# Second layer norm and routing written as one stage, chunk by chunk, in a two-layer transformer kernel with a mixture of experts

## The reference, cut to what matters

```python
xn = _layernorm(x, axis=-1)
x = x + _L0_attn_ref(xn, ...) + _L0_ffn_ref(xn, L0_ffn_W1, L0_ffn_W2, L0_ffn_W3)
xn = _layernorm(x, axis=-1)
x = x + _L1_attn_ref(xn, ...) + _L1_ffn_ref(xn, L1_ffn_Wr, ...)
# inside the second layer
v = (x @ Wv)
probs = jax.nn.softmax(x @ Wr, axis=-1)
topw, topi = jax.lax.top_k(probs, K)
pos = (jnp.cumsum(oh, axis=0) * oh).sum(-1) - 1
```

## Time and profile before

| | us |
|---|---|
| median of 3 runs | 2762.9 (2759.66 to 2764.67) |
| span of the profiled execution, first to last instruction | 2757.8 |
| TensorE busy in the span | 2526.8 (92%) |
| VectorE busy in the span | 1757.1 (64%) |
| from the end of the first feed-forward's last sum to the next block after routing | 1331.3 to 1428.2 |

### The profile page before, as it was taken

One profiled execution on the slowest core, in us unless ns is written; L12 is line 12 of the kernel. 1 busy time (PEld: TensorE's weight loads), 2 busy tenths in 40 slices (PEclk: granted clock), 3 DMA queues, 4 the chain that ended last, 5 costly groups with the idle time before them and its releaser, 6 DMA issues. The chain is left out here.

```text
span 2757.8 us, 35900 instructions
## 1 busy us (share of the span) xinstructions
PE 2526.8 (92%) x12212; PEld 1711.0 (62%) x12212; DVE 1757.1 (64%) x4109; ACT 1080.5 (39%) x2566; POOL 1022.2 (37%) x756
## 2 busy tenths in 40 slices
PE   5889989898869999999697999978999979999998
PEld 2334434343348888888575777756777656667886
DVE  4647757575435555555545999956999923335886
ACT  2125535353522333222223777725777721111111
POOL 2217758584911111110003676624445410001442
PEclk9969999999979999999899999999999999999999
DMA  7371211111020000000211101010000078883201
GB/s 252 131 180 24 54 24 40 26 35 31 2 106 16 16 15 15 15 16 1 85 50 54 62 29 28 23 40 24 9 9 16 1 259 295 295 294 93 58 24 62
DMA packets 167335, 193.64 MB, mean 70 GB/s; under 512 B 51982, under 2 KB 114446, under 8 KB 166784
## 3 DMA queue, kind: packets, MB, share of 16 engines
q1 hardware_dynamic: 155648, 178.90, 20.8%
q0 software_dynamic: 11520, 12.64, 1.4%
HBM read 161.95 MB, written 54.53 MB: 78 GB/s over the span
## 5 line engine op out<-in xcount | busy, mean ns | idle before, releaser
L621 DVE TENSOR_REDUCE mx<-bank 128x1 f32<-128x512 f32 x512 | 327.9, 679 | 121.7 <-PE bank L528 115.5
L468 POOL TENSOR_TENSOR probs<-probs 128x1024 f32<-128x1024 f32 x128 | 301.5, 2376 | 211.2 <-PE bank L551 174.0
L679 ACT ACTIVATE probs<-bank 128x1024 f32<-128x1024 f32 x256 | 250.1, 1022 | 271.8 <-PE bank L541 271.8
L1475 POOL TENSOR_SCALAR mix<-mix,sm 128x256 f32<-128x256 f32 (+1 forms) x256 | 232.5, 919 | 175.1 <-DVE sm L1372 174.9
L1415 ACT ACTIVATE ms<-ms,sm 128x256 f32<-128x256 f32 (+1 forms) x512 | 247.6, 486 | 93.9 <-DVE sm L1343 92.9
L528 PE MATMUL bank<-k_parts,q_parts 96*128 96x512 f32 x512 | 219.8, 476 | 7.3 <-DVE X L644 3.3
L528 PEld LDWEIGHTS bank<-k_parts,q_parts 96*128 96x128 f32 x512 | 94.0, 196 | 171.4 <-DVE mx L621 139.1
L855 POOL TENSOR_TENSOR up_lo<-up_raw,up_hi 128x1024 fp32r<-128x1024 f32 x16 | 46.2, 2907 | 401.0 <-ACT up_hi L845 401.0
L1343 DVE CUSTOM_DVE_ANT_0 ms<-bank,misc 128x256 f32<-128x256 f32 (+1 forms) x512 | 184.7, 399 | 2.3
L541 PE MATMUL bank<-q_parts,k_parts 97*128 97x512 f32 x512 | 148.4, 406 | 15.8 <-ACT probs L679 8.9
L925 DVE TENSOR_TENSOR hid<-bank,sg 128x512 f32<-128x512 f32 x64 | 44.2, 691 | 180.2 <-ACT sg L875 180.2
(11 more groups left out here) (221 smaller groups left out, 5863.4 us busy)
## 6 DMA issues: line engine op xcount, KB each, us to landing
ewg<-in_L_ffn_Wg_dram SPq DMA_DIRECT2D x32, 704.0 KB, 6.8
ewu<-in_L_ffn_Wu_dram SPq DMA_DIRECT2D x32, 704.0 KB, 8.0
ewd<-in_L_ffn_Wd_dram SPq DMA_DIRECT2D x32, 512.0 KB, 5.2
q_parts<-qk_dram SPq DMA_DIRECT2D x48, 256.0 KB, 4.4
up_raw<-in_L_ffn_W_dram SPq DMA_DIRECT2D x16, 512.0 KB, 4.1
ewd<-in_L_ffn_Wd_dram SPq DMA_DIRECT2D x32, 192.0 KB, 5.3
qk_dram<-qk_hi SPq DMA_DIRECT2D x4, 1280.0 KB, 5.1
qk_dram<-qk_lo SPq DMA_DIRECT2D x4, 1280.0 KB, 7.2
```

What stands on the lines that cost most here:

```text
L468: pool.tensor_tensor(probs[:, even, half, :], probs[:, even, half, :], probs[:, odd, half, :], ALU.add).then_inc(S["paired"], 1)
L621: dve.reduce_max(mx[:, U % 2, q, h:h + 1], bank[:, h, :], AX.X).then_inc(S["max"], 1)
L679: act.activation(probs[:, s % BUFS, 2 * x:2 * x + 2, :], bank[:, 2 + 2 * x:4 + 2 * x, :], ACT.Exp, scale=scale).then_inc(S["exps"], 1)
L1475: pool.tensor_scalar(mix[:, p % 2, h, 0:w], mix[:, p % 2, h, 0:w], sm[:, p % 3, 8 + h:9 + h], None, ALU.mult).then_inc(S["probs"], 1)
```

## The change

The code that both layer norms shared is split. `layer_norm0` is the first one, with the same instructions as before. The second is written into `normalise_and_route`, one block in place of two:

- The statistics and aggregates of the second layer norm go into `swiglu`, last column group of the first feed-forward: behind the sum of each chunk stand 4 statistics and 4 aggregates. The aggregates are kept in the columns of the constant `had`, which is no longer needed by then.
- Variance plus epsilon, square root and reciprocal are done in 4 pieces of 4 tiles.
- TensorE's order is by chunks: transposes of the chunk's 4 tiles, some value products, logits of the chunk, turning of the logits of the chunk before. Value products 0 to 12 stand ahead of the count, 13 to 15 behind it.
- Banks: transposes use 3 banks in place of 4, the logits one (bank 3) in place of 4, the value products 2 (6 and 7) in place of 4.
- The 4 MB store of the normalised rows is 4 stores of 1 MB.

The core of the diff:

```diff
+                if last and a == 1:
+                    for s in range(SUBS):
+                        wait(dve, S["added"], (i * 2 + a) * (NC * SUBS) + c * SUBS + s + 1)
+                        dve.bn_stats(stats[:, s, :], X[:, c * SUBS + s, :]).then_inc(env["ln"][0], 1)
+                    for s in range(SUBS):
+                        dve.wait_ge(env["ln"][0], NT + c * SUBS + s + 1)
+                        dve.bn_aggr(env["moments1"][:, c * SUBS + s, :], stats[:, s, :]).then_inc(env["ln"][1], 1)
...
+                def turn_rows(n):
+                    pe.wait_ge(xn_ready, NT + n + 1)
+                    if n >= 3:
+                        pe.wait_ge(xt_taken, NT + n - 2)
...
+                def logits(c):
+                    if c == 0:
+                        pe.wait_ge(router_high, 4)
+                    pe.wait_ge(xt_taken, NT + SUBS * (c + 1))
+                    pe.wait_ge(lgT_s, c)
...
+                n = 0
+                for c in range(NC):
+                    for s in range(SUBS):
+                        turn_rows(c * SUBS + s)
+                    while n < (0, 1, 3, 5)[c]:
+                        values(n)
+                        n += 1
+                    logits(c)
+                    if c:
+                        turn_logits(c - 1)
+                while n < 6:
                     values(n)
+                    n += 1
+                turn_logits(NC - 1)
+                while n < 13:
+                    values(n)
+                    n += 1
                 pe.wait_ge(cnt, 1)
-                pe.matmul(bank[:, 6, :], env["before"], mask[:, :, :], start=True, stop=True).then_inc(lg, 1)
-                pe.matmul(bank[:, 7, :], env["ones"], mask[:, :, :], start=True, stop=True).then_inc(lg, 1)
-                for n in range(6, NT):
+                pe.wait_ge(lg_s, 2)
+                pe.matmul(bank[:, 4, :], env["before"], mask[:, :, :], start=True, stop=True).then_inc(lg, 1)
+                pe.matmul(bank[:, 5, :], env["ones"], mask[:, :, :], start=True, stop=True).then_inc(lg, 1)
+                while n < NT:
                     values(n)
+                    n += 1
...
+                for c in range(NC):
+                    root(c)
+                act.wait_ge(router_in, 32)
+                act.wait_ge(router_high, 2)
+                act.activation(wrh[:, :, 0:E + 1], wr[:, :, :], ACT.Copy).then_inc(router_high, 1)
+                act.wait_ge(H["kw"], CREDIT + 16)
+                act.activation(wvh[:, :, :], wv[:, :, :], ACT.Copy).then_inc(H["khi"], 1)
+                for n in range(2 * SUBS):
+                    take_rows(n)
+                take_logits(0)
+                take_values(0)
+                for c in range(2, NC):
+                    for s in range(SUBS):
+                        take_rows(c * SUBS + s)
+                    take_values(2 * c - 3)
+                    take_values(2 * c - 2)
+                    take_logits(c - 1)
+                take_turned(0)
+                take_values(5)
+                take_logits(NC - 1)
+                take_turned(1)
+                for n in range(6, 13):
+                    take_values(n)
```

More of the change, by code:

```diff
@@ L140, in build, with layer_norm0 @@
                              wvh=sb(rows, "wv_hi", [P, KD, 4 * P], F32R), wvl=sb(rows, "wv_lo", [P, KD, 4 * P], F32R))
-                    layer_norm(env, "1", rows=r["xn"], r=r)
-                    route(env, r)
+                    normalise_and_route(env, r)
                 attention1(env, r)
             feed_forward1(env, r)
[L147 to L154, removed]
+def layer_norm0(env):
+    nc, X, bank, ident, sem = (env[k] for k in ("nc", "X", "bank", "ident", "sem"))
+    consts_loaded = sem("ln_consts0")
+    x_loaded = [sem(f"ln_x0_{c}") for c in range(4)]
+    env["ln"] = [sem("ln_" + n) for n in ("stats", "aggr", "var", "sd", "rstd", "xn", "xt", "taken")]
@@ L217, in _ @@
+        @block.sync
+        def _(sp):
+            src = env["ins"]["L0_attn_x"].rearrange("b (n p) d -> p (b n) d", p=P)
+            sp.dma_start(env["misc"][:, :], env["consts"]["misc"]).then_inc(consts_loaded, 16)
+            for c in range(QL):
+                n = NT // QL
+                sp.dma_start(X[:, c * n:(c + 1) * n, :], src[:, c * n:(c + 1) * n, :]).then_inc(x_loaded[c], 16)
         @block.vector
@@ L219, in _ @@
             for n in range(NT):
-                if first and n % (NT // QL) == 0:
+                if n % (NT // QL) == 0:
                     dve.wait_ge(x_loaded[n // (NT // QL)], 16)
@@ L255, in _ @@
         def _(act):
-            act.wait_ge(var_done, once + 1)
+            act.wait_ge(var_done, 1)
             act.activation(sd[:, 1, :], sd[:, 0, :], ACT.Sqrt).then_inc(sd_done, 1)
[L258 to L263, removed]
             for n in range(NT):
[L265 to L268, removed]
+                act.wait_ge(xt_ready, n + 1)
+                act.activation(env["xnT"][:, :, n * P:(n + 1) * P], bank[:, n % 4, :].rearrange("p (k t) -> p k t", k=KD),
+                               ACT.Copy).then_inc(xt_taken, 1)
 def wait(engine, signal, count):
@@ L1021, in _, with values @@
                     mm.then_inc(lg, 1)
-                pe.wait_ge(H["klo"], CREDIT + 1)
-                for n in range(6):
-                    values(n)
+                def values(n):
+                    if n == 0:
+                        pe.wait_ge(H["klo"], CREDIT + 1)
+                    pe.wait_ge(H["vtaken"], CREDIT + n - 1)
+                    for k in range(KD):
+                        for part, (x, w) in enumerate(((xh, wvh), (xh, wvl), (xl, wvh))):
+                            mm = pe.matmul(bank[:, 6 + n % 2, :], x[:, k, n * P:(n + 1) * P], w[:, k, :],
+                                           start=(k == 0 and part == 0), stop=(k == KD - 1 and part == 2))
+                    mm.then_inc(H["vrows"], 1)
@@ L1042, in _, with take_turned @@
-                for g in range(2):
+                    act.activation(logT[:, c * CH:(c + 1) * CH], bank[0:W, 3, :], ACT.Copy).then_inc(lgT_s, 1)
+                def take_turned(g):
                     act.wait_ge(lg, 2 * (g + 1))
```

224 lines of the change are left out of this document (119 added, 105 removed).

## The result

The changed kernel takes 2765.9 us (median of 20 runs, 2763.69 to 2770.27), the kernel before 2761.19 (20 runs, 2759.36 to 2765.07): ratio 1.0017, 95% interval 1.0011 to 1.0024. It is slower by 0.17%, 4.7 us. Forecast were 2766.4 and "within 0.2%".

The account below looks back on a forecast made before the run. VectorE, then TensorE, set the seam's pace: -6.3 statistics, +4.2 `wv`, +0.4 GpSimd, +0.3 new order, +5.4 bare tail, -0.5 switch: net +3.5 on span 2757.8, plus 5.1 to the median, 2766.4 us; range 2759 to 2772.5.

Parts of the forecast that it names:

- The likeliest case: Whole seam: tail bare and clock mostly held, 2766.4 us, within 0.2% of the kernel before; chance 60%.
- a joint's idle: TensorE at each chunk's start, waiting for the fourth tile's chain through ScalarE and VectorE: about 1.3 us idle.
- a logits wait: TensorE before logits 2, logits 3 and the last turning, waiting for ScalarE's logits copy: 1.5 us each.
- Part 1, the statistics: Twelve of sixteen statistics cost nothing behind feed-forward sums; first tile normalised at 1336.7 against 1343.01, 6.3 us gained.
- What is late next: ScalarE waits for the load of `wv` before taking any tile: of 6.3 us gained, 2.1 are left.
- The hold by GpSimd: GpSimd's 4.51 us subtraction holds VectorE's fourth normalising to 1347.9; 1.7 us of gain left, bounds 0 and 3.3.
- Part 2: TensorE's new order: first logits at half clock, 5.2 us, then 59.6 us to the count, starting at 1415.4.
- Part 3, the tail: VectorE's routing behind the count, covered by only three products, ends 5.4 us behind ScalarE's last copy.
- the first chunk's 5.7: Fourth normalising not held by GpSimd (-3.3) and first logits at full clock (-2.4); both give 2760.7.
- The clock rival: TensorE's clock falls at two or three chunk starts, costing 3.2 to 4.8 us: 2769.6 to 2771.2, slower; chance 25%.
- The row that spoke for it: Profile window 1352:1356: TensorE busy 4.00 of 4.00 us with transposes at granted clock 0.50, 1.2 GHz.
- The milder first chunk: VectorE not held by GpSimd or first logits at full clock: 2763.1 or 2764.0, both 2760.7; chance 10%.

Follow-up runs that it names:

- the second execution: The changed kernel run once more, unchanged, for one look: 2763.32 us, a single run.
- The order change of the first four tiles: Changed kernel with ScalarE taking the first four tiles before it rounds the value weights: 2758.5 us, ratio 0.9988 to the kernel before.
- the late subtraction: Changed kernel with GpSimd's subtraction started only after the seventh tile is normalised: 2762.62 us, ratio 1.0005 to the kernel before.
- ten products: Changed kernel with ten value products ahead of the count in place of thirteen: 2762.38 us, ratio 1.0004 to the kernel before.

## Why the prediction was right

The likeliest case came in, by its own steps. In us from the seam's start (the prediction's times less 1328.77), forecast and measured:

| step | forecast | measured |
|---|---|---|
| block opens | 5.5 | 5.5 |
| first tile normalised | 7.9 | 7.3 |
| ScalarE idle for `wv` | 4.5 | 3.22 (3.69 in the second execution) |
| first high part, behind `wv` | 14.0 | 13.7 |
| fourth normalising | 3.3 long | 3.74 long, 3.2 of it hold |
| first logits | 21.8 | 21.5 |
| twelve first logits | 5.2 | 4.4 (1353.82 to 1358.26) |
| a joint's idle, a logits wait | 1.3, 1.5 | 0.99, 1.31 (1.47 from start to start) |
| tail starts | 88.6 | 88.0 |
| tail ends | 102.6 | 102.1 |
| seam's end | 102.9 | 102.6 |

*Part 1, the statistics.* The cover in the feed-forward holds (0.30 of the gap is left). What arrives of the gain of 7 at the first normalising is 2.0 to 2.3 at the tiles (forecast: 2.1 of 6.3), in both kernels: by moving them alone, and by moving them back (2.8 at the seam's end).

*What is late next.* The order change of the first four tiles shows `wv` and the hold together as 7.8, the late subtraction shows the hold as 3.2 of these. The hold by GpSimd is shown as a cause, since nothing but its start was changed.

*Part 2.* The three waits for logits copies showed 3.84 of idle. Their removal is worth 3.74 from the seam's start and 4.35 from the second chunk's logits on, where the landing of `wv` plays no part. That is more than the idle: from the start of the matmul ahead of a logits wait to the start of the one behind it are 1.70 us (1375.66 to 1377.36), where neighbours are 0.23 apart. The forecast for the three was 4.6.

*Part 3, the tail.* It is worth 4.35 (4.65 from the second chunk's logits on), as the difference of two covers: the changed kernel ends with the tail 5.0 behind the last copy; with ten products the end is the last copy's.

*The size.* In the sum, the step "with 0.3 for the switch the next block opens at 1431.7, against 1428.24" was mis-sized: the forecast difference was 3.5, that of the medians is 4.7. That 2766.4 came so near to 2765.9 is in part luck: the sum started from a median of three runs, 2762.9, which is 1.7 above the median of twenty, and was 1.2 short in the difference, and the two nearly cancel. The changed side was right within 0.3. The side of before was not: its 1428.24, a seam of 99.50, is one execution, and of three the longest, since its logits ran at half clock for 6.2 us. The mean of the three is 98.1 and that of the two changed ones 102.7: 4.6, and that agrees with the medians. With so few executions this is a likely account and not a proof of the last microsecond. I had granted the clock's chance only to the changed kernel, as a rival; the row of 0.77 in the old logits was read as the old order's cost. The lower edge of its range, 2759, is not what the named terms give (2766.4 less the first chunk's 5.7 is 2760.7); nothing rested on it.

*The rivals.* The clock rival is off: at the joints the granted clock was 1.00, that is 2.4 GHz. The row that spoke for it, 0.50 at 1352:1356 under transposes, is half of a reading: TensorE went on with nothing but transposes, and from 1357.1 to 1364.0 the granted clock was 1.00 (the window at 1358:1363 above). So the transposes did not hold the clock down, and they were no evidence for a fall at the joints. The Trainium skill ("TensorE: Matmul & The Clock Gate", Part 4: PE-mode transpose) says that full clock does not engage for transposes; the window at 1358:1363 shows 1.00 under them, and the measurement decides. The milder first chunk is off as forecast: it was held, and the first logits began at half clock, though they took 0.8 less than twelve at half clock, because the clock rose at the eighth.

## What to carry to other kernels

Work that leaves the path uncovers what ran beneath it: here 10.7 us of statistics had hidden a weight load, a table load and a round of copies, and 2 of 7 us came through. Ask what was under the piece before you move it, and move that as well. When independent work is dealt out between a chain's steps, count what is left behind the last wait: the tail behind the count needs 14 us of cover, which is five products of 2.8 (worked out; six were run, and the end was then the last copy's). The changed order left three there and stacked seven where the chain needed four. And take the kernel before from several executions: a clock that is up in one and down in the next makes as much difference as the change.

## What the runs showed of the hardware

A subtraction on GpSimd stretched a VectorE normalising from 0.54 to 3.74 us, to 0.3 us behind its own end, while VectorE's subtraction from PSUM beside it took its usual 0.69 (at 1346.66, with GpSimd busy from 1346.22).

The granted clock rose to 1.00 (2.4 GHz) under nothing but transposes, in each of three executions of the kernel before, and stood there 6.8 us, 10.2 us and, in the third, on into the logits; in the window read closely TensorE was busy with transposes 3.28 of 5.00 us. Then, behind the same transposes and the same idle of 1.68 us, the first logits ran at 1.2 GHz in two of these executions (for 6.2 and 3.2 us) and at 2.4 GHz in the third. That is worth up to 2.8 us. The work on the engine alone does not tell which; what does is not shown.

Starts of the same instruction at mid-span lay from 1328.77 to 1334.41 in three executions of the kernel before, two of them (1331.91 and 1334.41) on one chip.
